# Shared-key attention on one core: scores, maxima products and masks issued in four column groups of 32

## The reference, cut to what matters

```python
q = (x @ Wq).reshape(Bsz, Tlen, H, D)     # 16 heads of 16
k = x @ Wk                                 # one head
v = x @ Wv                                 # one head
scores = jnp.einsum('bihd,bjd->bhij', q, k) / jnp.sqrt(jnp.float32(D))
scores = jnp.where(causal, scores, -jnp.inf)
attn = jax.nn.softmax(scores, axis=-1)
out = jnp.einsum('bhij,bjd->bihd', attn, v).reshape(Bsz, Tlen, C)
return out @ Wo + bo
```

## Time and profile before

| | |
|---|---|
| median of 3 runs | 1732.24 us (1724.12 to 1732.43) |
| profiled execution, its own time | 1730.56 us |
| its span in the trace | 1728.7 us |
| TensorE busy | 1624.0 us, 94% of the span |
| VectorE, ScalarE busy | 1038.1 us (60%), 790.5 us (46%) |
| mean granted TensorE clock | 0.969 of full |
| maxima products L1116 / masks L1118 | 211.1 to 662.3 us |
| scores L1144 / masks L1147 | 234.8 to 728.6 us |
| value products L1157 | 240.8 to 729.8 us |

### The profile page before, as it was taken

The page is one execution under the profiler, slowest core; times in us unless marked ns, Lnnn a source line. Parts: engine busy times, 40 slices in busy tenths (PEclk is TensorE's granted clock), DMA queues, the critical chain, the costliest instruction groups (busy, mean ns, idle before and its releaser), DMA issues.

```text
span 1728.7 us, 25533 instructions
## 1 busy us (share of the span) xinstructions
PE 1624.0 (94%) x9844; PEld 972.9 (56%) x9852; DVE 1038.1 (60%) x1867; ACT 790.5 (46%) x1797; POOL 366.9 (21%) x420
## 2 busy tenths in 40 slices
PE   7999879999999999999999889977999999999998
PEld 4666544433333334454566456765777777774556
DVE  4666577787787774533534774316777777952222
ACT  3331335657667776622111143316677767642110
POOL 2321000000100000400000023404555555640000
PEclk9999879999999999999999989987999999999999
DMA  5000220000000002010000030000000020000000
GB/s 179 2 2 21 60 75 2 2 1 2 1 1 2 1 1 77 27 50 0 16 0 0 1 118 5 1 6 1 8 1 7 1 83 2 2 1 0 13 13 25
DMA packets 28362, 34.98 MB, mean 20 GB/s; under 512 B 5713, under 2 KB 24722, under 8 KB 27730
## 3 DMA queue, kind: packets, MB, share of 16 engines
q1 hardware_dynamic: 28242, 33.35, 6.2%
HBM read 23.74 MB, written 2.10 MB: 15 GB/s over the span
## 4 chain that ended last, share of the span: by engine, by line
PE 82%; DVE 11%; ACT 3%; issue 3%; POOL 1%; DMA 0%; POOLq 0%; SPq 0%; DVEq 0%; ACTq 0%
PE PS L1157 8%; PE PS L1144 7%; PE PS L1116 7%; PE PS L1408 6%; PE PS L1414 6%; PE PS L2495 6%; PE PS L1436 6%; DVE arena L1325 4%; PE PS L2108 3%; PE PS L2484 3%; PE PS L2462 3%; PE PS L2078 2%; PE PS L339 2%; PE PS L2438 2%; PE PS L1193 2%
## 5 line engine op out<-in xcount | busy, mean ns | idle before, releaser
L1247 ACT ACTIVATE arena<-PS 128x512 f32<-128x512 f32 (+3 forms) x640 | 319.7, 534 | 175.9 <-PE PS L1144 77.7
L1325 DVE TENSOR_REDUCE arena<-PS 128x1 f32<-128x1024 f32 (+7 forms) x320 | 329.8, 1061 | 97.6 <-PE PS L1118 69.7
L1144 PE MATMUL PS<-arena 99*128 99x512 bf16 (+3 forms) x640 | 205.8, 353 | 1.4 <-ACT arena L1247 1.0
L1116 PE MATMUL PS<-arena 96*128 96x512 bf16 (+3 forms) x640 | 179.0, 358 | 18.3 <-DVE arena L1325 17.5
L1157 PE MATMUL PS<-arena 128*32 128x512 f32 (+3 forms) x1280 | 150.5, 542 | 2.8 <-ACT arena L1253 1.7
L190 POOL TENSOR_TENSOR rstd<-ve,mhalf 128x4 f32<-128x4 f32 x32 | 32.3, 1010 | 535.8 <-DVE ve L218 535.7
L1144 PEld LDWEIGHTS PS<-arena 99*128 99x128 bf16 x640 | 60.7, 99 | 147.4 <-ACT arena L1247 115.9
L185 ACT ACTIVATE XT<-PS 128x1024 f32<-128x1024 f32 x32 | 32.8, 1024 | 225.1 <-PE PS L178 225.1
L2603 ACT ACTIVATE arena<-arena 128x128 f32<-128x128 f32 x256 | 122.7, 484 | 1.3 <-DVE arena L2782 1.3
L2495 PE MATMUL PS<-arena 128*128 128x256 f32 x512 | 121.0, 379 | 0.2
L1408 PE MATMUL PS<-XT,arena 128*128 128x512 f32 x256 | 120.4, 592 | 0.1
(11 more groups left out here) (241 smaller groups left out, 2779.2 us busy)
## 6 DMA issues: line engine op xcount, KB each, us to landing
arena<-arena SPq DMA_DIRECT2D x55, 128.0 KB, 2.4
XT<-in_L_attn_xT SPq DMA_DIRECT2D x4, 512.0 KB, 8.7
X<-in_L_attn_x SPq DMA_DIRECT2D x4, 512.0 KB, 8.7
arena<-in_L_attn_out_w SPq DMA_DIRECT2D x1, 2048.0 KB, 7.3
out<-X SPq DMA_DIRECT2D x4, 512.0 KB, 2.9
arena<-in_dmask SPq DMA_DIRECT2D x1, 1024.0 KB, 5.7
arena<-in_L_ffn_W_up SPq DMA_DIRECT2D x1, 1024.0 KB, 5.4
arena<-in_L_ffn_W_gate SPq DMA_DIRECT2D x1, 1024.0 KB, 7.6
```

What stands on the lines that cost most here:

```text
L1116: last = pe.matmul(flat[:, o:o + w], q, a.KS[0:SROWS, CH * kc:CH * kc + w], start=True, stop=kc < c)
L1144: last = pe.matmul(PS[:, b, lo:CH], a.KS[0:rows, P * j:P * (j + 1)], a.QS[0:rows, G1 * g + r, CH * c + lo:CH * (c + 1)], start=True, stop= ...
L1247: act.activation(a.PB[:, n % 3, r, lo:CH], PS[:, 4 + x % 3, lo:CH], ACT.Exp, scale=D0 ** -0.5).then_inc(a.e2, 1)
L1325: dve.tensor_reduce(dst, src, AX.X, ALU.max, negate=True).then_inc(a.m1, 1)
```

## The change

Each product of `unit` and `score`, and each mask, was one MATMUL with 128 stationary columns. It becomes four MATMULs with 32 stationary columns each, into the matching 32 partitions of the same bank, with the same moving operand. The semaphore is raised by the last of the four. Waits, banks and order stay; `value`, `turn_maxima`, `sums`, `turn_inverse` and `out` stay as they are.

```diff
+COLUMNS1 = [slice(32 * p, 32 * p + 32) for p in range(4)]
...
@@ unit
-                last = pe.matmul(flat[:, o:o + w], q, a.KS[0:SROWS, CH * kc:CH * kc + w], start=True, stop=kc < c)
+                for p in COLUMNS1:
+                    last = pe.matmul(flat[p, o:o + w], q[:, p], a.KS[0:SROWS, CH * kc:CH * kc + w], start=True, stop=kc < c)
             if kc == c:
-                last = pe.matmul(flat[:, o + n - P:o + n], k.identb[:, :], a.mqb, start=False, stop=True)
+                for p in COLUMNS1:
+                    last = pe.matmul(flat[p, o + n - P:o + n], k.identb[:, p], a.mqb, start=False, stop=True)
@@ score
-        last = pe.matmul(PS[:, b, lo:CH], a.KS[0:rows, P * j:P * (j + 1)], a.QS[0:rows, G1 * g + r, CH * c + lo:CH * (c + 1)],
-                         start=True, stop=j < TPC * c)
+        keys = a.KS[0:rows, P * j:P * (j + 1)]
+        for p in COLUMNS1:
+            last = pe.matmul(PS[p, b, lo:CH], keys[:, p], a.QS[0:rows, G1 * g + r, CH * c + lo:CH * (c + 1)],
+                             start=True, stop=j < TPC * c)
         if j >= TPC * c:
-            last = pe.matmul(PS[:, b, lo:lo + P], k.identb[:, :], a.mkb, start=False, stop=True)
+            for p in COLUMNS1:
+                last = pe.matmul(PS[p, b, lo:lo + P], k.identb[:, p], a.mkb, start=False, stop=True)
```

## The result

The changed kernel takes 1706.66 us (median of 4 runs, 1705.4 to 1709.71), the kernel before 1728.18 us beside it (median of 4): a ratio of 0.9873, 95% interval 0.9844 to 0.9901. In a second comparison, 6 runs against 11, it was 0.9845 (0.9819 to 0.9871). The forecast was 1709, with a range of 1698 to 1739. The profiled execution took 1705.40 us, 25.2 less than the 1730.56 of the one before.

The account below looks back on a forecast made before the run. TensorE, through its changes of mode, was taken to bound the attention stage. Terms: 33.4 + 2.3 − 7.5 − 2.7 − 1.2 − 3 = 21.3 us gained, forecast 1709 us, range 1698 to 1739.

Parts of the forecast that it names:

- The bound: Attention stage: TensorE is never idle for most of it except for changes of mode; the other engines wait for it.
- The value products' switches: 160 value products: entry gaps of 0.09 us and exit gaps of 0.14 us go, gaining 33.4 us.
- The maxima transposes: Transposes at L1130, seemingly in four-group mode already: their switches go, gaining 2.3 us (0 to 3.0).
- New switches: 44 visits of sums, turn_inverse, out and last x transposes stay whole-array among four-group work: 7.5 us lost (5.3 to 10.6).
- The cover: After 22 of 32 sums and turn_inverse visits, a wait for VectorE hides the new switches; cost 5.3 us if fully.
- Overhead of rounds: 1792 products become rounds of four MATMULs: 1.5 ns each (bounds 0 and 5), 2.7 us lost.
- Rival B: Narrow products: every round shows its weight load, 47 us lost, 1756 us; chance 6%.
- Rival C: TensorE's instruction supply becomes the bound: 1722 us at 19.4 ns each, 1753 at 24; 12% shared with A near 20 ns, 8% above.
- Rival A: Attention stage: ScalarE and VectorE take over as bound and absorb the gain, 1724 to 1732 us; 12% shared with slower supply.
- added 3: Attention stage: waits of all kinds, about 20 us, grow by 3 us as bursts of units wait for VectorE more often.

Follow-up runs that it names:

- Experiments 1 to 3: Changed kernel with units back to whole-array products: 1750.94 us; with scores back instead: 1780.44 us; with two column groups of 64 for four of 32: 1738.92 us.
- experiment 5: Changed kernel with the products of the sums in four column groups too: 1705.23 us, ratio 0.9843 to the kernel before.
- experiment 4: Changed kernel with every 512-column product off the diagonal issued as two halves of 256 columns, weights loaded again: 1706.89 us, ratio 0.9859.
- Experiments 8 and 9: VectorE's reductions of the maxima over half of their columns, in the kernel before (1704.15 us) and in the changed kernel (1684.72 us).

## Why the prediction was right

*The bound.* TensorE, by its changes of mode: right. Experiments 1 to 3 show that the price belongs to the change of mode, since the time follows their number in both directions, and a kernel with narrow products of another grouping gains nothing. The size was right too, 21.3 us forecast against 21.5 between the medians and 25.2 between the profiled runs, but that it is so close is partly luck: as told at the end of this section, the terms as measured add up to more than the gain.

*The value products' switches*, 33.4 us expected. The two gaps went exactly as forecast (0.22 us, 0.86 to 0.88 us, and 2.61 to 2.63 us a block). Summed over the starts, entries shrank from 13.3 to 1.9 us, exits with the first round from 23.0 to about 0. That is some 34 us.

*The maxima transposes*, 2.3 us. They were in the four-group mode already: a mask is now followed by them after 0.06 us instead of 0.15. At 8 of the 14 in the stage both gaps went, at the other 6, which follow a wait or the inverse sums, only the one behind: 8 × 0.19 + 6 × 0.10 = 2.1 us. At some of them a wait for VectorE stands right behind, so not all of it need have counted.

*New switches*, 44 visits, 7.5 us between 5.3 and 10.6. From score to score a sums visit grew from 1.03 to 1.32 us, 0.29 rather than my 0.24: the first load of the sums started 0.22 us ahead of its product before (591.53 and 591.75) and now starts with it (572.88), and the load of the score behind no longer starts ahead either. In the starts the visits grew by 8 to 9 us. The cover that I took for 22 of 32 visits was there for most of the sums: experiment 5 took 0.85 us off each visit on TensorE, and the stage fell by 1.3 us in all. It was not there everywhere: blocks 97, 113 and 129, which hold such a visit, grew from 3.60 to 3.68 us. The visit's 0.29 less the value product's 0.23 gives 0.06 of these 0.08.

*Overhead of rounds*, 2.7 us expected; at 1 ns a round (experiment 4) 1792 rounds make 1.8.

*Rival B* (each load exposed, 47 us): refuted by the 0.44 us of two 512-column rounds. The rule of the Trainium skill (TensorE: Matmul & The Clock Gate, "The mechanism"), that loads overlap only when they go to another row group, does not hold here, since all four groups share their rows. The same section also lets a load run ahead when it goes to the background weight buffer; no run here tells whether that is how these loads are hidden. *Rival C* (supply of instructions): refuted to 20 ns over 460 us and 14 to 17 in blocks. *Rival A*: TensorE's waits longer than 0.15 us sum to 30.1 us before and 29.1 after, where I had put them at about 20 and added 3.

*What the sum does not show.* The block periods give the net: 87 of 159 fell by 0.19 to 0.27 us (18.8 us together), 8 by 0.15 to 0.19 (1.4), 32 by 0.05 to 0.15 (3.5), among them those where ScalarE sets the pace (block 83 went from 2.52 to 2.40 us, its four exponentials take 2.39); 30 by less than 0.05 or not at all, with a net loss of 1.1, mostly blocks with sums or output visits or waits for VectorE. Two blocks (9 and 10) fell by 1.9 us together, which I had not foreseen: in the profile of before, TensorE was granted half clock there (1.2 of 2.4 GHz) from 274.8 to 278.2 us. In the 6 us ahead it had waited three times for VectorE, 0.33 to 0.69 us each.

```profile
274.80:278.20 3.40, 3.40 (x24) 1.66 (x24) 1.37 (x4) 0.87 (x4) 1.40 (x5) 0.50 0.00 0
```

The changed kernel's stretch with the same work (275.02 to 278.52 us) is granted 1.00, though waits for VectorE (0.33 and 0.47 us) stand ahead of it too. With the 0.4 us that two such blocks gain elsewhere, some 1.5 us of the 24.5 are this clock (an estimate), and the change itself gave about 23 us. Experiments 8 and 9, whose block 10 takes 2.12 and 1.88 us, give 22.6. The forecast's 21.3 is close to that, but my terms as measured (34 + 2 − 8 − 2 + 1) come to 27. The 4 us between are not settled. Waits under 0.15 us that I did not count may hold them; no run isolates them.

## What to carry to other kernels

Read the distance between starts across every change of the array's grouping, and count the changes: here each showed a gap of 0.09 to 0.14 us and cost 0.07 to 0.12 us of the stage, 350 of them about 2% of the kernel. A stretch of mixed work should be in one grouping, and one that is changed by half is worse than either. Before making a further piece of the bound engine's queue faster, look at what waits behind it: the sums' visits lost 0.85 us each and gave 0.1, because VectorE was being waited for.

## What the runs showed of the hardware that was not expected

*Column groups run at their own pace.* The 12-column transposes use one group only. In the changed kernel the score behind them starts in the other three while they still run:

```profile
408.66 0.24 PE L1155 MATMUL PS<-arena,identb 128*32 128x128 bf16 x4
408.72 0.27 PE L1135 MATMUL PS<-identb,arena 128*12 128x128 bf16 x2
408.78 0.34 PE L1151 MATMUL PS<-arena 99*32 99x384 bf16 x3
408.83 0.27 PE L1135 MATMUL PS<-identb,arena 128*12 128x128 bf16 x2
408.94 0.33 PE L1151 MATMUL PS<-arena 99*32 99x384 bf16 x1
408.95 0.37 PE L1155 MATMUL PS<-arena,identb 128*32 128x128 bf16 x4
```

Three of the score's MATMULs start at 408.78, between the transposes, and the fourth at 408.94. By the code the transposes write the first 32 partitions, so the fourth is that of their own group; the trace does not name the groups. Starts are thus not always in the order of the queue, which the description of the kernel took for granted.

Nothing shows that time was gained by it. The four masks of the last row stretch over 0.37 us instead of 0.23, because one of them starts at 409.11, after its own group's score. From the first transpose that makes 0.39 us, where in the earlier trace rows it was 0.32 and a score of 384 columns, 0.48 us together: the group with the transposes gained the 0.09 us of a gap and no more, and TensorE then waits for VectorE until 409.95.

The order matters for the semaphore, which the last-issued MATMUL of a product raises. Here that MATMUL ends at 409.18, before the one that lags (409.33), and yet the semaphore is updated at 409.37 and the exponential of this bank starts at 409.45. It is the same at all 14 visits of the transposes in the stage: the update comes 39 to 40 ns after the modelled end of the MATMUL that lags. So in these runs the semaphore of the last-issued one still stood for all four.

*Small whole-array products start at the pace of their loads.* The eight MATMULs of the sums stream 4 columns each and start 0.11 us apart, as their loads of 128 float32 columns do; in four groups, with loads of 32 columns, all 32 start within 0.25 us. That the load is what is paid is read from this, not isolated.
